# A decoder layer on one core: PSUM banks of the late steps, and the places of the router's parts and of a batch's first scores

## The chip, the cores and the metric

The kernel runs on one core of a Trainium2 chip, as one program. The metric is the device time of one execution in microseconds (us); lower is better. The engines are TensorE (PE in the profile; PEld is its weight load), VectorE (DVE), ScalarE (ACT), GpSimd (POOL) and SyncE (SP), which issues the DMAs. PSUM, in which PE writes and from which DVE and ACT read, has eight banks of 512 fp32 per partition; the kernel holds them as `bank[:, 0..7, :]`.

## What is computed

One layer over 8 sequences ("batches") of 512 rows by 256 features, each with a context of 1024 rows by 128:

```python
x = layernorm(x + attn(x))              # conv over the sequence, 16 heads, softmax of 512x512 scores in bf16
x = layernorm(x + xattn(x, ctx))        # 16 heads: causal self attention + cross attention to ctx, fp32
x = layernorm(x + ffn(x))               # a router over 64 tiles:
#   cluster = argmax(calibrate(x @ cluster_sigs.T)); tile = argmax(calibrate(x @ sigs.T)[cluster])
#   comp = tanh(gelu(x @ cw1 + cb1) @ cw2 + cb2)
#   hh = relu(comp @ w1[tile] + b1[tile]); mag = hh @ w2[tile] + b2[tile]
#   y = layernorm(x + mag * directions[tile] * scale) * gamma + beta
```

## The kernel before

Each engine runs its own program, written out by hand; semaphores tie them. A batch b goes through the stages below, and batches follow one another in a loop (batches 1 to 5 share one body). The router of a batch runs inside the next one (c = b - 1); `tail` does it for the last. What an engine does, and in which order, is the order of the calls in its `batch`.

**Opening: first attention, heads h = 0 to 15.** PE makes four score tiles a head (`scores1`, banks 0 to 3), DVE copies them with their minimum (L712), ACT takes the exps (`exp1`, L565), DVE and ACT scale rows (`norm1`), a DMA transposes them (`transpose1`), PE multiplies with the values (`pv1`, five heads later). `keep_clock` issues filler matmuls (L1263) that nobody reads. Among the heads lie the end of the previous batch (y's transposes `heads_to_features` L1170, the output projection `second_out`, the second norm), the router's first part (`tokens_to_features`, `route`, ACT's `gate_exps` and `hidden`), the context's keys and values (`context_key`, `values`), and DVE's convolution for batch b + 1 (`convolve`, L674 to L679).

**Transition and lead.** Output projection, first norm, the first matmuls of batch b + 1, then twelve projections `unit(u)` for the 16 self and cross heads (four groups of four heads), and between them the first seven sets of row maxima, m = 0 to 6. DVE does the router's gates and choices here.

**Steps s = 0 to 47.** Step s is a block of 128 keys for a group of four heads: 16 self steps, then 32 cross steps. In a step PE issues four transposed scores (`scoresT`, L1402, L1405; one for each row group of 32), ACT takes their exps (L617), and every four steps PE multiplies a "burst" with the values (`pv`, L1420); from burst 9 on it is cut in halves, behind steps s % 4 = 2 and s % 4 = 0. DVE finds the row maxima (`maxima`, L976, L979) some steps ahead, adds them as a row to the queries (`put_rows`, L1001), and copies and divides the results (`outputs` L991, L994; `finish` L1009 to L1015). The maxima end with step 36; the steps from there on are called the late stretch here.

**Banks in the steps.** Banks 0 to 3 are a ring for all that DVE reads: `slot_uses` numbers the uses in PE's order, use n lies in bank n % 4, and PE may write it when use n - 4 is released (`slot_out`). Banks 4 to 7 are ACT's: score n lies in bank 4 + n % 4, and PE waits until exp n - 4 is out (`pT_ready`).

**The router's last part.** `expert_columns` (PE transposes the chosen experts behind step 35, DVE copies them), `gather` behind step 40 (PE: compression L1204, parameters L1208, directions L1213), DVE's `compressed`, ACT's tanh (`compress`), DVE's `spline` (L841 to L852), the norms (`third_sums` to `last_norm`), and SP's `store`. Its scratch lies in q_s and k_s, and so ACT's first projection waits for the previous store (`out_dma`). Behind the last step stand three filler matmuls (L1462).

## Time and profile before

| | us |
|---|---|
| median of 3 runs | 2655.57 |
| lowest and highest | 2650.71, 2660.38 |
| the profiled execution | 2660.13 |
| its span, first to last instruction | 2658.0 |

Busy in the span: PE 2439.8 us (92%), DVE 1924.3 (72%), ACT 1364.6 (51%), POOL 193.6 (7%). The mean granted clock of PE is 0.948. In the timelines, a row gives the start from the span's first instruction, the time to the end of the last of its x instructions, the engine and line, output <- inputs, shape, and in brackets how long the engine stood before it and what released it. An fp32 matmul has two records, so four scores are "x8". Line numbers are those of the kernel before, in `order` rows of the changed kernel those of the changed one.

### The profile page before, as it was taken

Reading aid. Unit: us, or ns where it says so; the run is one execution under the profiler, and the core shown is the slowest. Engines: PE = TensorE matmul, PEld = TensorE weight load, DVE = VectorE, ACT = ScalarE, POOL = GpSimd, SP = SyncE. Lnnn points to the kernel's source line nnn. Section 1 sums busy time; section 2 is a strip of 40 time slices with the busy share of each in tenths; the row PEclk is TensorE's granted clock in tenths of the full one; section 3 lists DMA queues with packets and bytes.
Section 4 is the critical chain, followed back from the end, with each engine's and each line's share of the span. In section 5 each row is a group of like instructions: output and inputs, shape, how many; then the busy total and the mean of one; then the engine's idle time right before and its main releaser. Section 6 shows DMA issues by size and latency. Waiting matters only on the chain.

```text
span 2658.0 us, 44424 instructions
## 1 busy us (share of the span) xinstructions
PE 2439.8 (92%) x13522; PEld 1148.8 (43%) x13554; DVE 1924.3 (72%) x5302; ACT 1364.6 (51%) x2937; POOL 193.6 (7%) x353
## 2 busy tenths in 40 slices
PE   6999989999999989999899998999989999879994
PEld 2454334543445433454335543355434444334432
DVE  6868477884878858687587866878578785668854
ACT  3635564454734648246482465734556355654550
POOL 2010001100011000110001100010000100001000
PEclk8999999998999989999899998999989998999985
DMA  5400032000520006000050001500024000330000
GB/s 138 84 9 1 1 81 55 1 1 9 96 40 1 2 9 119 17 2 1 20 117 9 2 1 47 90 9 1 1 49 79 9 1 1 68 60 1 1 9 8
DMA packets 250899, 83.20 MB, mean 31 GB/s; under 512 B 236064, under 2 KB 246432, under 8 KB 250656
## 3 DMA queue, kind: packets, MB, share of 16 engines
q1 hardware_dynamic: 250656, 80.20, 14.8%
q8 instruction: 123, 2.02, 0.3%
q14 instruction: 120, 0.98, 0.1%
HBM read 17.27 MB, written 4.19 MB: 8 GB/s over the span
## 4 chain that ended last, share of the span: by engine, by line
PE 79%; DVE 11%; issue 4%; ACT 3%; DMA 2%; DVEq 0%; POOL 0%; SPq 0%; ACTq 0%; POOLq 0%
PE bank L1371 18%; PE bank L1131 14%; PE bank L1420 12%; PE bank L1405 10%; PE bank L1367 4%; PE bank L1402 4%; DVE work L712 3%; PE bank L1263 3%; PE bank L1240 2%; PE bank L1227 2%; PE bank L1293 2%; PE bank L1384 2%; DMA work<-work 1%; PE bank L1431 1%; ACT work L617 1%
## 5 line engine op out<-in xcount | busy, mean ns | idle before, releaser
L617 ACT ACTIVATE work<-bank 128x512 f32<-128x512 f32 (+3 forms) x1536 | 744.0, 552 | 669.6 <-PE bank L1405 335.1
L979 DVE TENSOR_REDUCE top_half<-bank 128x1 f32<-128x512 f32 x1024 | 625.6, 682 | 18.5 <-PE bank L1371 18.5
L1371 PE MATMUL bank<-k_c,q_c 32*128 32x512 f32 x2048 | 630.5, 631 | 0.0
L1405 PE MATMUL bank<-q_c,k_c 32*128 32x512 f32 x2048 | 584.4, 656 | 23.2 <-ACT work L617 22.3
L565 ACT ACTIVATE work<-work,neg 128x512 bf16<-128x512 bf16 x512 | 362.2, 711 | 25.5 <-DVE work L712 24.6
L1371 PEld LDWEIGHTS bank<-k_c,q_c 32*128 32x128 f32 x2048 | 273.1, 183 | 226.8 <-DVE top_half L979 140.6
L712 DVE TENSOR_SCALAR_CACHE_REDUCE work<-bank 128x512 bf16<-128x512 f32 x512 | 322.0, 686 | 60.6 <-PE bank L1227 60.5
L1420 PE MATMUL bank<-work,v_flat 128*32 128x512 f32 (+3 forms) x3072 | 341.8, 583 | 19.1 <-ACT work L617 17.3
L1405 PEld LDWEIGHTS bank<-q_c,k_c 32*128 32x128 f32 x2048 | 245.5, 188 | 131.1 <-ACT work L617 70.5
L976 DVE CUSTOM_DVE_ANT_0 masked<-bank,mask_w 128x384 bf16<-128x384 f32 (+3 forms) x512 | 222.7, 488 | 67.3 <-PE bank L1367 60.1
L1402 PE MATMUL bank<-q_s,k_s 32*128 32x512 f32 (+3 forms) x1024 | 261.5, 468 | 0.0
L1420 PEld LDWEIGHTS bank<-work,v_flat 128*32 128x32 f32 x3072 | 91.7, 114 | 261.3 <-issue 149.0
L1367 PE MATMUL bank<-k_s,q_s 32*128 32x128 f32 (+3 forms) x1024 | 183.2, 475 | 0.0
L1227 PE MATMUL bank<-k,q 32*128 32x512 bf16 x512 | 144.9, 388 | 27.2 <-DVE work L712 20.8
L1402 PEld LDWEIGHTS bank<-q_s,k_s 32*128 32x128 f32 x1024 | 145.1, 183 | 13.3 <-ACT work L617 7.6
L1263 PE MATMUL bank<-k,identb 128*128 128x512 bf16 x544 | 145.7, 406 | 2.8 <-issue 1.6
L1240 PE MATMUL bank<-work,v 128*32 128x512 bf16 x512 | 133.5, 383 | 15.8 <-DMA work<-work 14.0
L994 DVE TENSOR_TENSOR featA<-bank,featA 128x512 f32<-128x512 f32 x32 | 22.1, 692 | 167.9 <-PE bank L1420 154.7
L1367 PEld LDWEIGHTS bank<-k_s,q_s 32*128 32x128 f32 x1024 | 100.1, 183 | 76.5 <-DVE top_s L976 32.9
L903 DVE TENSOR_SCALAR work<-work,rden 128x512 bf16<-128x512 bf16 x400 | 120.9, 360 | 4.5
L504 POOL TENSOR_SCALAR_AFFINE_SELECT work<-work 128x512 f32<-128x512 f32 x128 | 81.6, 637 | 557.3 <-ACT work L617 557.3
L991 DVE COPY featA<-bank 128x512 f32<-128x512 f32 x64 | 44.3, 692 | 104.6 <-PE bank L1420 104.3
(201 smaller groups left out, 2499.7 us busy)
## 6 DMA issues: line engine op xcount, KB each, us to landing
xT_pad<-xT SPq DMA_DIRECT2D x16, 256.0 KB, 2.8
ctx_sb<-ctxT SPq DMA_DIRECT2D x8, 512.0 KB, 3.5
x_res<-x SPq DMA_DIRECT2D x8, 512.0 KB, 4.9
out<-k_s SPq DMA_DIRECT2D x8, 512.0 KB, 2.9
work<-work SPq DMA_TRANSPOSE x112, 4.3
qk_sb<-qkT SPq DMA_DIRECT2D x1, 512.0 KB, 4.7
wq_sb<-Wq SPq DMA_DIRECT2D x1, 512.0 KB, 6.6
wk_sb<-Wk SPq DMA_DIRECT2D x1, 512.0 KB, 7.0
```

The costliest lines, as they stand in the source:

```text
L565: nc.scalar.activation(e1[:, h % E1_SLOTS, t, :], s1[:, h % 2, t, :], ACT.Exp, bias=neg1[:, h % 2, t:t + 1], scale=-1.0, accum_out=den1[:, ...
L617: nc.scalar.activation(pT[:, s % PT_SLOTS, g, q0:S], bank[:, RING + n % EXP_RING, 0:S - q0], ACT.Exp, scale=SCALE).then_inc(pT_ready, 1)
L712: nc.vector.tensor_scalar(s1[:, h % 2, t, :], bank[:, (NT * h + t) % A1_BANKS, :], -SCALE, None, ALU.mult, ALU.min, accum_out=neg1[:, h % ...
L976: nc.vector.tensor_tensor_reduce(masked[:, g, 0:n], scores[:, 0:n], mask_w[:, S - n:S], -1.0, -MASKED, ALU.add, ALU.min, top_s[:, i % 2, u ...
L979: nc.vector.tensor_reduce(top_half[:, i % 2, g, u // 2, u % 2:u % 2 + 1], scores, AX.X, ALU.max, negate=True).then_inc(slot_out, 1)
L1131: last = mm(dst, lhsT(k), rhs(k), start=(k == 0), stop=(k == tiles - 1))
L1263: mm(bank[:, at, :], identb[:], k_1[:, 0, :], start=True, stop=True)
L1367: mm(dst[:, 0:n], q_s[rows, i, P * u:n], k_s[rows, i, 0:n], start=True, stop=True, tile_position=(GW * g, 0)).then_inc(slot_in, 1)
L1371: mm(dst, q_c[rows, i, P * t:P * (t + 1)], k_c[rows, i, S * half:S * (half + 1)], start=True, stop=True, tile_position=(GW * g, 0)).then_i ...
L1402: mm(dst[:, 0:S - q0], k_s[rows, i, q0:q0 + P], q_s[rows, i, q0:S], start=True, stop=True, tile_position=(GW * g, 0)).then_inc(sT_mm, 1)
L1405: mm(dst, k_c[rows, i, P * u:P * (u + 1)], q_c[rows, i, :], start=True, stop=True, tile_position=(GW * g, 0)).then_inc(sT_mm, 1)
L1420: last = mm(dst[GW * g:GW * (g + 1), q0:S], v_flat[:, at:at + GW], pT[:, s % PT_SLOTS, g, q0:S], start=(s % BURST == 0), stop=(s % BURST = ...
```

## The change

- From step 37 on (`LATE_STEP`) the ring of DVE is banks 0 and 1 (`LATE_RING`), and the exps use banks 4, 5, 6, 7, 2, 3 (`LATE_EXP_BANKS`, `exp_bank`); `free_slot` and `scoresT` wait accordingly.
- The compression gets a place of its own in the opening: PE at head 8 in bank 5, DVE at 7, ACT's tanh at 9. Expert columns go behind maxima 4 of the lead, the gather and DVE's spline behind maxima 6, the expert choice from maxima 2 to 1. The sums and norms start at step 39. The scratch moves to xs, o1T and r_sb; DVE waits for the store before the second norm, and ACT no longer does.
- A batch opens with the scores of heads 0 and 1; y's transposes, the output projection, the second norm, the router's parts, keys and values follow one or more heads later. The residual is loaded behind head 3. The filler matmuls at a batch's end go; head 7 gets eight fillers instead of four.
- `convolve(b + 2)` stands at step 42 of DVE's program instead of `convolve(b + 1)` in the opening; `convolve(1)` in front of batch 0.

```diff
-    EXPERT_STEP, GATHER_STEP = 35, 40
+    EXPERT_LEAD, GATHER_LEAD = 4, 6
...
+    LATE_STEP = 37
+    LATE_RING, LATE_EXP_BANKS = 2, (4, 5, 6, 7, 2, 3)
...
+        comp = sb("comp", [P, NT, 2])[:]
...
-        z_sb = k_flat[:, 0:NT * D].rearrange("p (t d) -> p t d", t=NT)
+        z_sb = xs_flat.rearrange("p (t d) -> p t d", t=NT)
...
+                if ffn and m == EXPERT_LEAD:
+                    order.append(("expert",))
+                if ffn and m == GATHER_LEAD:
+                    order.extend(("gather", i) for i in range(3))
             for s in range(ALL_STEPS):
+                if s == LATE_STEP:
+                    late = len(order)
...
-                if ffn and s == EXPERT_STEP:
-                    order.append(("expert",))
-                if ffn and s == GATHER_STEP:
-                    order.extend(("gather", i) for i in range(3))
...
-            return {name: n for n, name in enumerate(order)}
+            return {name: n for n, name in enumerate(order)} | {"late": late}
...
+        def slot(uses, use):
+
+            return bank[:, use % RING if use < uses["late"] else (use - uses["late"]) % LATE_RING, :]
...
+        FIRST_LATE = GH * LATE_STEP
+
+        def exp_bank(n):
+            return bank[:, RING + n % EXP_RING if n < FIRST_LATE else LATE_EXP_BANKS[(n - FIRST_LATE) % len(LATE_EXP_BANKS)], :]
...
-                sp.dma_start(out[c].rearrange("(t p) d -> p t d", p=P), z_sb).then_inc(out_dma, 16)
+                sp.dma_start(out[c].rearrange("(t p) d -> p t d", p=P), r_sb[:]).then_inc(out_dma, 16)
...
-                    if h == 1:
+                    if h == 3:
...
-                    if prev:
-                        act.wait_ge(out_dma, FIRST + (b - 1) * 16)
...
-                        nc.scalar.activation(pT[:, s % PT_SLOTS, g, q0:S], bank[:, RING + n % EXP_RING, 0:S - q0], ACT.Exp,
+                        nc.scalar.activation(pT[:, s % PT_SLOTS, g, q0:S], exp_bank(n)[:, 0:S - q0], ACT.Exp,
...
-                if prev:
-                    y_features(0, featA, c)
...
                     if prev:
-                        if h == 2:
+                        if h == 0:
+                            y_features(0, featA, c)
+                        if h == 4:
                             y_features(1, featB, c)
-                        if h == 4:
+                        if h == 5:
                             gate_exps(c)
-                        if h == 5:
+                        if h == 6:
                             hidden(c)
-                    if 0 <= h - 7 < CTX_UNITS:
-                        context_key(h - 7)
+                        if h == 9:
+                            compress(c)
+                    if 0 <= h - 8 < CTX_UNITS:
+                        context_key(h - 8)
...
-                    if prev and s == GATHER_STEP + 2:
-                        compress(c)
...
-            def compressed(c, base, uses):
-                dve.wait_ge(slot_in, base + uses["gather", 2] + 1)
-                nc.vector.tensor_tensor(comp_in, slot(uses["gather", 0])[:, 0:2 * NT].rearrange("p (t i) -> p t i", t=NT),
+                nc.vector.tensor_copy(expertT, slot(uses, use)[0:TILES, :]).then_inc(slot_out, 1)
+
+            def compressed(c):
+                dve.wait_ge(comp_mm, c + 1)
+                nc.vector.tensor_tensor(comp, bank[:, 5, 0:2 * NT].rearrange("p (t i) -> p t i", t=NT),
                                         cb2_row[:].unsqueeze(1).broadcast_to([P, NT, 2]), ALU.add).then_inc(comp_b, 1)
...
-                param = slot(uses["gather", 0])[:, 2 * NT:2 * NT + NT * PARAMS].rearrange("p (t n) -> p t n", t=NT)
+                dve.wait_ge(slot_in, base + uses["gather", 2] + 1)
+                param = slot(uses, uses["gather", 0])[:, 0:NT * PARAMS].rearrange("p (t n) -> p t n", t=NT)
...
                 ln_apply(2, c, lambda t: nc.vector.scalar_tensor_tensor(
-                    z_sb[:, t, :], z_sb[:, t, :], ln_r[:, 2, t:t + 1], r_sb[:, t, :], ALU.mult, ALU.add))
+                    r_sb[:, t, :], z_sb[:, t, :], ln_r[:, 2, t:t + 1], r_sb[:, t, :], ALU.mult, ALU.add))
...
                 scores1(b, 0)
                 scores1(b, 1)
-                if ahead:
-                    convolve(b + 1)
-                if prev:
-                    second_residual(c, sf)
...
                     if prev:
                         if h == 0:
+                            second_residual(c, sf)
+                        if h == 1:
+                            dve.wait_ge(out_dma, FIRST + (b - 1) * 16)
                             second_norm(c)
-                        if h == 5:
+                        if h == 6:
                             router_scores(c)
-                    if h in (6, 8, 10, 12):
-                        values((h - 6) // 2)
+                        if h == 7:
+                            compressed(c)
+                    if h in (7, 9, 11, 13):
+                        values((h - 7) // 2)
...
                     maxima(m)
                     if prev and m == 0:
                         local_gates(c, sf)
-                    if prev and m == 2:
+                    if prev and m == 1:
                         expert_choice(c, sf)
+                    if prev and m == EXPERT_LEAD:
+                        expert_columns(base, uses)
+                    if prev and m == GATHER_LEAD:
+                        spline(c, sf, base, uses)
                 for s in range(ALL_STEPS):
-                    if prev and s == GATHER_STEP + 1:
-                        compressed(c, base, uses)
-                    if prev and s == GATHER_STEP + 2:
-                        spline(c, sf, base, uses)
+                    if prev and s == LATE_STEP + 2:
                         third_sums(c, sf)
-                    if prev and s == GATHER_STEP + 4:
+                    if prev and s == LATE_STEP + 4:
                         third_norm(c)
-                    if prev and s == GATHER_STEP + 5:
+                    if s == LATE_STEP + 5 and ahead == 2:
+                        convolve(b + 2)
+                    if prev and s == LATE_STEP + 6:
                         last_sums(c, sf)
-                    if prev and s == GATHER_STEP + 6:
+                    if prev and s == LATE_STEP + 8:
                         last_norm(c)
...
-                    if prev and s == EXPERT_STEP:
-                        expert_columns(base, uses)
...
+            convolve(1)
             batch(0, prev=False)
...
+            def free_slot(base, uses, use):
+
+                late = uses["late"]
+                if use >= late + LATE_RING:
+                    pe.wait_ge(slot_out, base + use - LATE_RING + 1)
+                elif use >= late:
+                    pe.wait_ge(slot_out, base + late)
+                elif use >= RING:
                     pe.wait_ge(slot_out, base + use - RING + 1)
-                return slot(use)
+                return slot(uses, use)
...
+            def compressed(c):
+                pe.wait_ge(gelu_done, c + 1)
+                for t in range(NT):
+                    last = mm(bank[:, 5, 2 * t:2 * t + 2], hT[:, P * t:P * (t + 1)], cw2_sb[:], start=True, stop=True)
+                last.then_inc(comp_mm, 1)
...
             def gather(c, base, uses):
-                pe.wait_ge(gelu_done, c + 1)
-                dst = free_slot(base, uses["gather", 0])
-                for t in range(NT):
-                    mm(dst[:, 2 * t:2 * t + 2], hT[:, P * t:P * (t + 1)], cw2_sb[:], start=True, stop=True)
+                dst = free_slot(base, uses, uses["gather", 0])
                 pe.wait_ge(slot_out, base + uses["expert",] + 1)
                 for t in range(NT):
-                    at = 2 * NT + PARAMS * t
-                    last = mm(dst[:, at:at + PARAMS], expertT[:, P * t:P * (t + 1)], table[:, D:TABLE], start=True, stop=True)
+                    last = mm(dst[:, PARAMS * t:PARAMS * (t + 1)], expertT[:, P * t:P * (t + 1)], table[:, D:TABLE], start=True, stop=True)
...
                 if prev:
-                    heads_to_features(c)
...
                     elif prev:
-                        pe.wait_ge(gelu_done, b)
+                        pe.wait_ge(comp_b, b)
...
                 scores1(0)
                 scores1(1)
                 if prev:
-                    second_out(c)
+                    heads_to_features(c)
                 keep_clock(7, FILLERS)
                 for h in range(2, H):
                     scores1(h)
                     if h >= 5:
                         pv1(h - 5)
                     if prev:
-                        if h == 3:
+                        if h == 2:
+                            second_out(c)
+                        if h == 5:
                             tokens_to_features(c)
-                        if h == 4:
+                        if h == 6:
                             route(c)
-                    if h in (7, 9, 11, 13):
-                        values((h - 7) // 2)
-                    if 0 <= h - 8 < CTX_UNITS:
-                        context_key(h - 8)
+                        if h == 8:
+                            compressed(c)
+                    if h in (8, 10, 12, 14):
+                        values((h - 8) // 2)
+                    if 0 <= h - 9 < CTX_UNITS:
+                        context_key(h - 9)
                     if h < 13:
-                        keep_clock(7 if h < 4 else 6, FILLERS if h < 7 else FILLERS // 2)
+                        keep_clock(7 if h < 6 else 6, FILLERS if h < 8 else FILLERS // 2)
+                context_key(CTX_UNITS - 1)
...
-                    if n >= EXP_RING:
+                    if n >= FIRST_LATE + len(LATE_EXP_BANKS):
+                        pe.wait_ge(pT_ready, b * ALL_SCORES + n - len(LATE_EXP_BANKS) + 1)
+                    elif n >= FIRST_LATE + EXP_RING:
+                        pe.wait_ge(slot_out, base + uses["late"])
+                    elif n >= EXP_RING:
                         pe.wait_ge(pT_ready, b * ALL_SCORES + n - EXP_RING + 1)
-                    dst = bank[:, RING + n % EXP_RING, :]
+                    dst = exp_bank(n)
...
+                    if prev and m == EXPERT_LEAD:
+                        expert_columns(c, base, uses)
+                    if prev and m == GATHER_LEAD:
+                        gather(c, base, uses)
...
-                    if prev and s == EXPERT_STEP:
-                        expert_columns(c, base, uses)
-                    if prev and s == GATHER_STEP:
-                        gather(c, base, uses)
                 pv(ALL_STEPS // BURST - 1, SECOND_HALF)
                 o_transpose(CROSS, HG - 1)
-                for _ in range(3):
-                    mm(bank[:, 7, :], ident[:], k_c[:, 0, 0:S], start=True, stop=True)
```

Besides, each call of `slot` and `free_slot` gets the table of uses as an argument, and `tail` is reordered alike.

The end of one batch and the opening of the next in PE's program (L1431, L1449: last transposes; L1170, L1178: y's transposes and r_sb's; L1227, L1237: first scores; L1263, L1273: fillers). Before:

```order
L1431 MATMUL bank<-ident,featA 128x128 x4
L1462 MATMUL bank<-k_c,ident 128x512 x3
L1489 REGISTER_ALU
L1489 COMPARE_AND_BRANCH
L1170 MATMUL bank<-ident,y_sb 128x128 x8
L1227 MATMUL bank<-k,q 128x512 x8
L1131 MATMUL bank<-wp_sb,featA 128x256 x8
L1263 MATMUL bank<-k,identb 128x512 x8
L1227 MATMUL bank<-k,q 128x512 x4
L1263 MATMUL bank<-k,identb 128x512 x8
L1227 MATMUL bank<-k,q 128x512 x4
```

Changed:

```order
L1449 MATMUL bank<-ident,featA 128x128 x4
L1506 REGISTER_ALU
L1506 COMPARE_AND_BRANCH
L1237 MATMUL bank<-k,q 128x512 x8
L1178 MATMUL bank<-ident,y_sb 128x128 x8
L1273 MATMUL bank<-k,identb 128x512 x8
L1237 MATMUL bank<-k,q 128x512 x4
L1134 MATMUL bank<-wp_sb,featA 128x256 x8
L1273 MATMUL bank<-k,identb 128x512 x8
L1237 MATMUL bank<-k,q 128x512 x4
L1273 MATMUL bank<-k,identb 128x512 x8
L1237 MATMUL bank<-k,q 128x512 x4
```

The scores of two heads stand ahead of y's transposes, the output projection is behind head 2, the fillers L1462 are gone.

The lead's end in PE's program, between the maxima of set 6 (128x384) and of step 0 (128x512). Before:

```order
L1137 REGISTER_ALU
L1367 MATMUL bank<-k_s,q_s 128x384
L1137 REGISTER_ALU
L1367 MATMUL bank<-k_s,q_s 128x384
L1137 REGISTER_ALU
L1367 MATMUL bank<-k_s,q_s 128x512
L1392 REGISTER_ALU
L1402 MATMUL bank<-q_s,k_s 128x512
L1137 REGISTER_ALU
```

Changed:

```order
L1145 REGISTER_ALU
L1381 MATMUL bank<-k_s,q_s 128x384
L1145 REGISTER_ALU
L1218 MATMUL bank<-table,featB 128x65 x4
L1145 REGISTER_ALU
L1223 MATMUL bank<-table,featB 128x256 x2
L1145 REGISTER_ALU
L1223 MATMUL bank<-table,featB 128x256 x2
L1145 REGISTER_ALU
L1381 MATMUL bank<-k_s,q_s 128x512
L1406 REGISTER_ALU
L1420 MATMUL bank<-q_s,k_s 128x512
```

The gather (L1218, L1223) stands between set 6 and the first maxima of step 0. In DVE's program the spline (here its end, L848 to L852) stands at the same place:

```order
L848 TENSOR_TENSOR o1T<-bank,o1T 128x4
L849 REGISTER_ALU
L850 TENSOR_SCALAR o1T<-o1T,scale_col 128x4
L32 REGISTER_ALU
L852 SCALAR_TENSOR_TENSOR xs<-bank,o1T,r_sb 128x256 x4
L32 REGISTER_ALU
L972 REGISTER_ALU
L977 ISA masked,top_s<-bank,mask_w 128x512
L977 ISA top_s 128x1
```

Step 40 in PE's program: scores, a half burst of values, and what is behind it. Before:

```order
L1405 MATMUL bank<-q_c,k_c 128x512
L1420 MATMUL bank<-work,v_flat 32x512 x8
L1137 REGISTER_ALU
L1204 MATMUL bank<-cw_sb,sig_work 128x2 x4
L1208 MATMUL bank<-table,featB 128x65 x4
L1137 REGISTER_ALU
L1213 MATMUL bank<-table,featB 128x256 x4
L1397 REGISTER_ALU
L1405 MATMUL bank<-q_c,k_c 128x512
L1397 REGISTER_ALU
```

Changed:

```order
L1423 MATMUL bank<-q_c,k_c 128x512
L1429 REGISTER_ALU
L1438 MATMUL bank<-work,v_flat 32x512 x8
L1411 REGISTER_ALU
L1423 MATMUL bank<-q_c,k_c 128x512 x2
L1411 REGISTER_ALU
L1423 MATMUL bank<-q_c,k_c 128x512
L1411 REGISTER_ALU
L1423 MATMUL bank<-q_c,k_c 128x512
```

The gather is gone from there, and of the next step's scores the first two follow each other without a wait of their own.

## Rows read from the trace of the kernel before

**Rows 1.** First line of the profile's page: span and instructions.
```profile
span 2658.0 us, 44424 instructions
```

**Rows 2.** Stretches: length, busy PE, PEld, DVE, ACT, POOL, PE clock, DMA share, GB/s.
```profile
291.00:339.00 48.00, 41.83 (x238) 13.80 (x235) 8.90 (x16) 24.26 (x48) 0.00 (x0) 0.89 0.00 1
...
611.00:664.00 53.00, 47.22 (x248) 17.28 (x241) 19.14 (x54) 22.50 (x45) 2.80 (x4) 0.81 0.03 11
...
1581.00:1630.00 49.00, 42.28 (x252) 15.78 (x242) 19.47 (x54) 22.36 (x46) 2.80 (x4) 0.93 0.03 12
...
458.00:500.00 42.00, 40.99 (x244) 20.95 (x244) 31.13 (x137) 15.70 (x32) 6.56 (x14) 1.00 0.05 14
```

**Rows 3.** Timeline of PE, late stretch of batch 0: start, us, what [idle before].
```profile
301.26 3.23 PE L1420 MATMUL bank<-work,v_flat 128*32 128x512 f32 x16
...
310.67 1.14 PE L1405 MATMUL bank<-q_c,k_c 32*128 32x512 f32 x8
...
312.53 2.59 PE L1405 MATMUL bank<-q_c,k_c 32*128 32x512 f32 x8 [0.73 <-ACT work L617]
...
315.05 1.92 PE L1420 MATMUL bank<-work,v_flat 128*32 128x512 f32 x16
...
334.37 3.39 PE L1420 MATMUL bank<-work,v_flat 128*32 128x512 f32 x16 [2.21 <-ACT work L617]
...
339.05 2.74 PE L1462 MATMUL bank<-k_c,ident 128*128 128x512 f32 x6
```

**Rows 4.** Timeline of ACT, a late cycle of batch 0.
```profile
311.88 4.03 ACT L617 ACTIVATE work<-bank 128x512 f32<-128x512 f32 x8 [2.21 <-PE bank L1405]
```

**Rows 5.** Timelines of DVE and PE: last maxima, and fillers behind a batch.
```profile
291.57 2.48 DVE L979 TENSOR_REDUCE top_half<-bank 128x1 f32<-128x512 f32 x4
...
608.79 2.47 DVE L979 TENSOR_REDUCE top_half<-bank 128x1 f32<-128x512 f32 x4
...
2540.80 2.46 DVE L979 TENSOR_REDUCE top_half<-bank 128x1 f32<-128x512 f32 x4
...
664.07 2.74 PE L1462 MATMUL bank<-k_c,ident 128*128 128x512 f32 x6
...
2594.33 4.43 PE L1462 MATMUL bank<-k_c,ident 128*128 128x512 f32 x6
```

**Rows 6.** Timeline of PE, the gather of batch 1.
```profile
628.20 1.05 PE L1204 MATMUL bank<-cw_sb,sig_work 64*128 64x2 f32 x8
...
629.11 1.08 PE L1208 MATMUL bank<-table,featB 64*128 64x65 f32 x8
...
630.03 2.15 PE L1213 MATMUL bank<-table,featB 64*128 64x256 f32 x8
```

**Rows 7.** Timeline of DVE, the opening of batch 1.
```profile
339.54 0.42 DVE L1011 TENSOR_TENSOR y_tmp<-bank,rec 128x256 f32<-128x256 f32 x1
...
343.02 0.69 DVE L712 TENSOR_SCALAR_CACHE_REDUCE work<-bank 128x512 bf16<-128x512 f32 x1 [2.59 <-PE bank L1227]
...
347.91 0.48 DVE L674 TENSOR_SCALAR xs<-xT_pad,conv_sb 128x512 f32<-128x512 f32 x1
...
351.86 1.28 DVE L742 TENSOR_TENSOR x_res<-x_res,bank 128x512 f32<-128x512 f32 x2
```

**Rows 8.** Timeline of PE, the opening of batch 1.
```profile
357.10 0.38 PE L1227 MATMUL bank<-k,q 32*128 32x512 bf16 x1 [2.93 <-DVE work L712]
...
379.62 1.03 PE L1227 MATMUL bank<-k,q 32*128 32x512 bf16 x4
```

**Rows 9.** Timeline of DVE, first maxima of step 0 in batch 1.
```profile
483.63 0.69 DVE L976 CUSTOM_DVE_ANT_0 masked<-bank,mask_w 128x512 bf16<-128x512 f32 x1
```

**Rows 10.** Timeline of DVE, first and last instruction of batch 1's spline.
```profile
636.41 0.23 DVE L841 TENSOR_TENSOR q_s<-bank,q_s 128x64 f32<-128x64 f32 x1 [4.02 <-ACT q_s L555]
...
638.65 1.66 DVE L852 SCALAR_TENSOR_TENSOR k_s<-bank,q_s,r_sb 128x256 f32<-128x256 f32 x4
```

**Rows 11.** Timeline of PE, the compression behind batch 7.
```profile
2631.64 1.86 PE L1204 MATMUL bank<-cw_sb,sig_work 64*128 64x2 f32 x8
```

59 lines of the change are left out of this document (24 added, 35 removed).

## The prediction

> **What bounds the kernel now.** I read first the page's span, then busy time by stretches, then the timelines of PE, DVE and ACT inside one batch, stage by stage. Eight batches share 2658.0 us [rows 1], one about 323 us. A batch has four stages with different limits. In the opening (16 first heads) PE, DVE and ACT feed each other. In the transition and the lead (projections and the first maxima) PE is the limit until projection 11 is out, then DVE. In steps 0 to 36 DVE's maxima are the limit. In the late stretch, from the last maxima to the end, nobody is full: ACT is busy 24.3 of 48 us in batch 0 and 22.5 of 53 us in batch 1, DVE 8.9 and 19.1, and PE's granted clock (1.00 is 2.4 GHz) falls to 0.89 and 0.81 on average [rows 2]. This is where the change aims, so I read it at single groups.
>
> In batch 0, at full clock, two late steps are a cycle: four scores back to back at 310.67, four more at 312.53 that each wait for a bank (2.59 us instead of 1.14), a half burst of values at 315.05. ACT's eight exps take 4.03 from 311.88 on, after 2.21 of idle: **6.24 us per two steps**, the same in each cycle at full clock [rows 3, 4]. A row group of PE needs about 1.06 us for one score (two passes), four run side by side, so a score that is released late costs its whole length before the values may start.
>
> From the start of the last four maxima to the start of the three L1462 fillers, this stretch is 339.05 - 291.57 = 47.5 us in batch 0, 664.07 - 608.79 = 55.3 in batch 1, 53.5 in batch 7 [rows 3, 5]; over the seven batches that carry the router it is 52.8 on average (50.2 to 55.3).
>
> **The change, part by part.** All per batch; there are seven batches with a router behind them.
>
> *Six banks for the exps.* With six, two of the second four scores start at once, the other two when ACT has freed the banks of the first two: ACT starts 1.21 us after the first score and takes 0.504 per exp [rows 3, 4], so the banks are free at 1.21 + 0.58 + 0.07 = 1.86 and 2.36, and the last score ends at 2.36 + 1.06 = 3.42. The half burst needs the first step's exps, done at 1.21 + 4 x 0.504 + 0.17 = 3.40. So it starts at 3.42 and the next cycle 1.86 later, at **5.28: 0.96 saved** per two steps. Five cycles (steps 37 to 46): **-4.8**. Ends: 0 if the values still start where they did, and 6.24 - 4.03 = 2.2 per cycle (-11) if ACT became the limit, which PE's order doesn't allow. VectorE's two ring banks cost nothing by the order: six ring uses are left, spread over eleven steps, and each finds its predecessor's predecessor copied some 5 us before.
>
> *The router's gather leaves step 40.* In batch 1 PE spends 628.20 to 632.1 on it, in front of the next scores [rows 6]: **-3.9**. The tanh and VectorE's part there lie in idle time.
>
> *The clock.* Where PE has stood or starved, the granted clock halves: the half burst takes 3.23 us at 301.26 against 1.92 at 315.05 [rows 3]. Batch 0 loses 4.2 us to that: 1.3 there and 1.5 in each of its last two half bursts (3.38 and 3.39). So its late stretch at full clock would be 43.3, and with the cycles 38.5. I take 2.1 us as left, for the waits before the last burst (2.2 us of idle, [rows 3]), which stay. So the stretch becomes **40.6**: -12.2 from 52.8, -6.9 in batch 0. The clock's share is about 3.5; the ends are 0 and 5.6 saved.
>
> The Trainium skill ("TensorE: Matmul & The Clock Gate", "A second HAM failure mode: psum-queue depth-cycling") says that cycling through PSUM banks with small idles between matmul groups makes the clock swing. The rows agree in kind: most slow pieces lie in this stretch. Taken fully, it would leave no loss, and the stretch would be 38.5.
>
> *The opening.* Now: last transposes, fillers, y's transposes, scores. DVE's first copy in batch 1 comes 3.06 us after the end of y_tmp (339.54 + 0.42 to 343.02) [rows 7], in the others 3.7 to 4.9. The change puts the scores first, which need only y_tmp: first copy at about +0.9. The convolution (347.91 to 351.86, 3.95 us [rows 7]) leaves DVE's path, and with it a wait of PE of 2.93 us [rows 8]; it lands at step 42, where DVE idles. But PE's list from the first scores to those of head 7 stays some 30 us (7 score groups of 0.96, 6 x 8 fillers of 1.87 per eight, second output 3.8, transposes 2.8, router 3.9, values 1.9), and 5 us of waits among heads 2 to 5 remain, because router and second norm are now one head later in the same chain: head 7 at +35.9, before 379.62 - 339.96 = +39.7 [rows 7, 8]. At its end the last context key now waits for ACT to pass head 14's exps, and gives back 1.4. Compression adds 1.05 on PE, in place of a wait that it fills. Net **-3** in batches 1 to 6, -1 in batch 7 (it had no convolution); ends -6 and +1. In batch 0 the convolution moves in front of the first head: +2.
>
> *The lead.* This is the bill. DVE has no slack once projections are out: from the middle of maxima 5 on its work is back to back, and step 0's maxima start at 483.63 [rows 9]. The change puts there the copy of the expert columns (0.6), and behind maxima 6 the spline, 636.41 to 640.31 = 3.9 us [rows 10]. The gather's second part takes PE 3.2 (1.08 + 2.15 [rows 6]) behind the scores of maxima 6, while DVE has only 1.9 us of maxima to do: DVE idles about 1.9. And step 0's maxima need the slots which the spline empties, so PE can't run ahead. 0.5 + 1.9 + 3.9 + 0.1 = 6.4, less 0.6 for the copy that leaves step 35. PE idles 2 to 4 us there; a piece at half clock after it costs me 1.2. Sum **+7**; ends +4 (the gather hidden) and +21 (below). The earlier expert choice and the dropped wait for the output lie where PE is the limit: 0.
>
> *The end.* After batch 7 the fillers, 4.43 us from 2594.33 on [rows 5], no longer delay y's transposes; y itself is complete some 1.5 us after their start (in batch 0 at 340.4 against 339.05 [rows 3, 7]): -2.8. The compression (2631.64, 1.86 at half clock) goes behind other waits: -1.9; the tanh's exchange -0.3 [rows 11]. **-5**.
>
> Sum: 7 x (-12.2 + 7) - 6.9 + 2 - 19 - 5 = **-65 us**. The profiled execution took 2660.1 us (span 2658.0), the median of the three runs is 2655.6: so 2595 and **2590**.
>
> **The rivals.**
> 1. *The clock holds everywhere* (0.2). Stretch at 38.5 (-14.3), lead at +5.8, opening -4: 7 x -12.5 - 9 + 2 - 5 = -100: 2556. For it: batch 4 had 0.93 there with all its waits [rows 2]. Against: the wait before the last burst stays.
> 2. *The lead eats it* (0.25). The late stretch gives 8 (gather, half the cycle's gain, no clock), the opening 1, the lead costs 7: 7 x -2 - 12 = -26: 2630. If the banks do nothing at all, because the half bursts start where they did, the stretch gives 4.5 and the time is about 2650, within the bound of no change.
> 3. *Slower* (0.05). PE's idle behind the gather halves its clock through steps 0 to 3. PE has no slack there either (busy 41.0 of the 42 us from 458 to 500 [rows 2]), so over the 14.4 us from 483.6 to 498 a halved clock makes it the limit and doubles them: lead +21. Against -15.2 from the rest it is 7 x 6 - 10 = +32: 2688. It decides from a lead cost of about 16.6. Against: the slow pieces of the late stretch are single half bursts with full ones behind them [rows 3].
>
> The skill's same page ("Why this matters for your kernels") advises against gaps between matmul bursts. That speaks against dropping the fillers and against the gather's place; by it, rival 3's piece would appear behind the gather in each batch, while I book 1.2.
>
> **How the numbers follow.** Forecast 0.5, between 2570 and 2615. Rivals as above. The range 2550 to 2640 takes in rival 1 and most of rival 2. A measurement can tell 0.3% (8 us) from no change: faster 0.87, same 0.07, slower 0.06.
>
> **What would show it.** Late cycles: ACT's groups of eight 5.3 us apart instead of 6.24, and two of the second four scores without a wait. Clock in the late stretch above 0.9. In the lead, an idle of DVE of 2 us before the spline and the first step's maxima some 6 us later after the last projection. Head 7's scores 36 us after y_tmp. It is wrong if DVE's late block (third norm, convolution, sums) holds a ring slot for which a half burst waits, or if the last context key delays the transposes by more than 1.4.

## The result, and the profile after

The changed kernel takes 2639.55 us (median of 7 runs, 2633.86 to 2640.67), the kernel before 2660.38 (7 runs beside them, 2650.71 to 2666.49): ratio 0.9919, 95% interval 0.9900 to 0.9938. It is faster by 21 us. I had forecast 65, at 2590; the measured time lies just inside the upper edge of my range.

The profiled execution has a span of 2631.8 us against 2658.0 [rows 1]. Where the 26 us come from, worked out from the timelines of DVE and ACT between fixed events, as a mean over the seven batches that carry a router (us). "y_tmp" is the last of the four in a batch, "the featB copy" is ACT's copy behind the first attention. The late stretch ends here at y_tmp; in the prediction it ended at the fillers, about 1 us earlier.

| stage | before | after | forecast of the change |
|---|---|---|---|
| opening: end of y_tmp to the featB copy | 105.3 | 108.5 | -3 |
| transition, to the first maxima | 13.6 | 13.5 | 0 |
| lead: first maxima to first cross maxima | 46.6 | 55.1 | +7 |
| steps, to the last top_c | 105.5 | 105.2 | 0 |
| late stretch, last top_c to the end of y_tmp | 51.3 | 36.7 | -12.2 |
| sum of one batch | 322.2 | 319.1 | -8.2 |
| all of batch 0 | 340.0 | 332.3 | -4.9 |
| behind batch 7 | 62.7 | 66.0 | -5 |

7 x (-3.1) - 7.7 + 3.3 = -26. The late stretch gained more than forecast, the lead cost more, and the opening and the program's end went the other way.

**The late stretch.** Stretches of the changed kernel (columns as in [rows 2]): the late stretches of batches 0, 1 and 4, and the lead of batch 1.

```profile
292.30:332.30 40.00, 36.20 (x244) 12.02 (x236) 14.09 (x26) 24.26 (x48) 0.00 (x0) 1.00 0.04 14
608.40:649.10 40.70, 36.91 (x244) 12.25 (x237) 23.11 (x55) 24.26 (x48) 2.79 (x4) 0.95 0.09 28
1575.60:1616.90 41.30, 37.50 (x244) 12.13 (x236) 23.04 (x55) 24.26 (x48) 2.79 (x4) 0.96 0.08 27
448.70:490.00 41.30, 39.77 (x174) 20.72 (x175) 28.43 (x119) 11.33 (x21) 6.85 (x17) 0.88 0.05 14
```

The granted clock there was 0.89, 0.81 and 0.93 [rows 2] and is 1.00, 0.95 and 0.96; the lead stood at 1.00 before and is now at 0.88. ACT's timeline in the late stretch of batch 2:

```profile
947.24 4.03 ACT L616 ACTIVATE work<-bank 128x512 f32<-128x512 f32 x8 [1.76 <-PE bank L1423]
952.44 4.03 ACT L616 ACTIVATE work<-bank 128x512 f32<-128x512 f32 x8 [1.18 <-PE bank L1423]
957.64 4.03 ACT L616 ACTIVATE work<-bank 128x512 f32<-128x512 f32 x8 [1.18 <-PE bank L1423]
962.84 4.03 ACT L616 ACTIVATE work<-bank 128x512 f32<-128x512 f32 x8 [1.18 <-PE bank L1423]
```

Groups of eight start 5.20 us apart, with 1.18 of idle instead of 2.21 [rows 4]: forecast 5.28 instead of 6.24. In the late stretches of the seven router batches before, late scores waited 30 times for ACT to free a bank, 19.6 us in all; in the changed kernel one such wait of 0.2 is left, and PE waits nowhere there for a ring slot.

**The seam between batches.** PE's timeline from batch 2 to 3 (the loop jumps there) and from 5 to 6 (the loop is left); y_tmp ends at 974.38 and 1937.75:

```profile
972.98 0.65 PE L1449 MATMUL bank<-ident,featA 128*128 128x128 f32 x4 [0.89 <-DVE featA L995]
976.92 3.83 PE L1237 MATMUL bank<-k,q 32*128 32x512 bf16 x8 [3.29 <-issue]
980.68 1.97 PE L1178 MATMUL bank<-ident,y_sb 128*128 128x128 f32 x8
982.44 3.62 PE L1273 MATMUL bank<-k,identb 128*128 128x512 bf16 x8
...
1937.81 3.62 PE L1237 MATMUL bank<-k,q 32*128 32x512 bf16 x8 [0.81 <-DVE y_tmp L1012]
```

At the jump PE stands 2.5 us longer and waits for nothing that the profile shows ("issue"). In both places the scores and what follows run at half clock: eight scores take 3.83 and 3.62 (four at full clock: 1.03), fillers that take 1.9 take 3.62.

**The lead.** PE and DVE around the gather, batch 3:

```profile
1121.02 1.10 PE L1218 MATMUL bank<-table,featB 64*128 64x65 f32 x8
1121.96 2.80 PE L1223 MATMUL bank<-table,featB 64*128 64x256 f32 x8
1124.69 1.22 PE L1381 MATMUL bank<-k_s,q_s 32*128 32x512 f32 x1
1124.80 0.23 DVE L841 TENSOR_TENSOR o1T<-bank,comp 128x64 f32<-128x64 f32 x1 [2.47 <-PE bank L1223]
```

DVE idles 2.47 us (1.6 to 1.7 in batches 2, 6 and 7, 2.8 to 3.0 in 1, 4 and 5; forecast 1.9), and the scores behind it take 1.22 instead of 0.69. Of the lead's +8.5, some 4.5 lie in front of the first exps (L616) and 4 between these and the first cross maxima (22.0 to 26.1 on average, the granted clock there 1.00 to 0.85). That second piece, in batches 2 and 3:

```profile
801.60:833.30 31.70, 30.70 (x175) 20.27 (x176) 21.32 (x83) 12.57 (x30) 4.45 (x7) 0.68 0.00 1
1126.80:1151.80 25.00, 25.00 (x175) 16.41 (x176) 20.32 (x79) 12.39 (x30) 4.44 (x7) 0.87 0.01 1
```

The other five batches have a clock of 0.87 to 0.89 there. Batch 2 goes the way of my rival 3, in one batch of seven: a clock of 0.68 makes that piece 31.7 us instead of 25.

**Behind batch 7.** PE's second output, and DVE up to the local gates:

```profile
2569.10 5.91 PE L1134 MATMUL bank<-wp_sb,featA 128*128 128x256 f32 x16 [1.10 <-ACT featA L539]
...
2587.99 0.42 DVE L751 COPY sig_raw<-bank 128x256 f32<-128x256 f32 x1 [7.25 <-ACT gates L543]
2592.82 0.17 DVE L825 TENSOR_TENSOR comp<-bank,cb_row 128x8 f32<-128x8 f32 x1 [4.41 <-PE bank L1211]
2599.70 0.18 DVE L765 TENSOR_SCALAR gates<-gates 128x32 f32<-128x32 f32 x1 [0.39 <-ACT gates L548]
```

DVE now waits 4.41 us for the compression in front of the cluster gates. The second output starts 3.3 us after y_tmp instead of 5.5, and loses that again: 5.91 us instead of 3.69.

### The profile page after: what moved, and what is told of

Same layout as the page of the kernel before. It is cut to its first block, busy times and chain, and to the rows that moved or that the text cites. A ratio compares the mean times of both kernels' runs of the same rounds, so it can differ in the third digit from the quotient of the medians.

```text
span 2631.8 us, 44428 instructions
## 1 busy us (share of the span) xinstructions
PE 2424.1 (92%) x13538; PEld 1145.0 (44%) x13538; DVE 1930.6 (73%) x5302; ACT 1366.1 (52%) x2937; POOL 192.9 (7%) x353
## 4 chain that ended last, share of the span: by engine, by line
PE 79%; DVE 10%; ACT 5%; issue 5%; DVEq 0%; DMA 0%; ACTq 0%; POOL 0%; SPq 0%; POOLq 0%
PE bank L1385 18%; PE bank L1134 15%; PE bank L1438 12%; PE bank L1423 9%; PE bank L1381 5%; PE bank L1420 3%; PE bank L1273 3%; PE bank L1237 3%; ACT work L566 3%; DVE work L711 3%; PE bank L1250 3%; PE bank L1302 2%; PE bank L1449 1%; PE bank L1398 1%; PE bank L1178 1%
## 5 line engine op out<-in xcount | busy, mean ns | idle before, releaser
L616 ACT ACTIVATE work<-bank 128x512 f32<-128x512 f32 (+3 forms) x1536 | 745.4, 552 | 620.0 <-PE bank L1420 323.0
L1423 PE MATMUL bank<-q_c,k_c 32*128 32x512 f32 x2048 | 553.0, 630 | 0.2 <-ACT work L616 0.2
L1438 PE MATMUL bank<-work,v_flat 128*32 128x512 f32 (+3 forms) x3072 | 319.6, 551 | 17.4 <-ACT work L616 17.3
L1420 PE MATMUL bank<-q_s,k_s 32*128 32x512 f32 (+3 forms) x1024 | 288.7, 522 | 0.0
L1423 PEld LDWEIGHTS bank<-q_c,k_c 32*128 32x128 f32 x2048 | 229.2, 183 | 96.9 <-ACT work L616 63.0
L1381 PE MATMUL bank<-k_s,q_s 32*128 32x128 f32 (+3 forms) x1024 | 217.1, 514 | 4.2 <-DVE o1T L848 3.1
L1237 PE MATMUL bank<-k,q 32*128 32x512 bf16 x512 | 155.3, 404 | 41.9 <-DVE work L711 21.0
L1420 PEld LDWEIGHTS bank<-q_s,k_s 32*128 32x128 f32 x1024 | 159.3, 202 | 15.6 <-ACT work L616 7.1
L1273 PE MATMUL bank<-k,identb 128*128 128x512 bf16 x608 | 164.7, 413 | 0.0
L1381 PEld LDWEIGHTS bank<-k_s,q_s 32*128 32x128 f32 x1024 | 115.8, 201 | 90.2 <-issue 38.0
```

Source lines behind the costliest of these rows:

```text
L616: nc.scalar.activation(pT[:, s % PT_SLOTS, g, q0:S], exp_bank(n)[:, 0:S - q0], ACT.Exp, scale=SCALE).then_inc(pT_ready, 1)
L1237: mm(bank[:, n % A1_BANKS, :], q_1[rows, i, P * t:P * (t + 1)], k_1[rows, i, :], start=True, stop=True, tile_position=(GW * (h % GH), 0)). ...
L1273: mm(bank[:, at, :], identb[:], k_1[:, 0, :], start=True, stop=True)
L1381: mm(dst[:, 0:n], q_s[rows, i, P * u:n], k_s[rows, i, 0:n], start=True, stop=True, tile_position=(GW * g, 0)).then_inc(slot_in, 1)
L1420: mm(dst[:, 0:S - q0], k_s[rows, i, q0:q0 + P], q_s[rows, i, q0:S], start=True, stop=True, tile_position=(GW * g, 0)).then_inc(sT_mm, 1)
L1423: mm(dst, k_c[rows, i, P * u:P * (u + 1)], q_c[rows, i, :], start=True, stop=True, tile_position=(GW * g, 0)).then_inc(sT_mm, 1)
```

## The experiments

Each was timed in three rounds beside the kernel before; the profiles are compared stage by stage as above. The runs of one kernel lie 1.4 to 25 us apart, so a difference of medians under some 10 us counts only with the stages beside it. All medians (us), and ratios to the kernel before with 95% intervals:

| run | what it is | median | ratio |
|---|---|---|---|
| e1 | change without the six banks | 2697.8 | 1.0145 (1.0113 to 1.0176) |
| e2 | change with the old opening | 2606.0 | 0.9806 (0.9775 to 0.9838) |
| e3 | before, new opening, early compression and late convolution | 2662.3 | 1.0013 (1.0001 to 1.0025) |
| e4 | change, fillers at the batch's end | 2641.6 | 0.9937 (0.9904 to 0.9970) |
| e5 | e2, convolution in the opening | 2613.0 | 0.9841 (0.9800 to 0.9883) |
| e6 | change, last context key later | 2630.5 | 0.9900 (0.9862 to 0.9937) |
| e7 | change, loop written out | 2633.0 | 0.9898 (0.9863 to 0.9933) |
| e8 | e2, router's last part late in three pieces | 2551.0 | 0.9602 (0.9561 to 0.9643) |
| e9 | e8, keys and values one head later | 2566.0 | 0.9647 (0.9627 to 0.9667) |
| e10 | e8, no fillers at the batch's end | 2557.1 | 0.9616 (0.9595 to 0.9636) |
| e11 | e2, spline waits for the first piece only | 2570.5 | 0.9673 (0.9647 to 0.9699) |
| e12 | e8, convolution in the opening | 2562.7 | 0.9633 (0.9609 to 0.9658) |
| e13 | e8, whole new opening | 2591.4 | 0.9745 (0.9709 to 0.9780) |
| e14 | e8, first half of the new opening | 2563.7 | 0.9636 (0.9599 to 0.9673) |
| e15 | e8, scores ahead of y's transposes | 2563.6 | 0.9646 (0.9611 to 0.9681) |
| e16 | e8, compression late behind batch 7 | 2545.2 | 0.9577 (0.9542 to 0.9612) |

### What each of the three parts is worth: e1, e2, e3, e12

e1:
```diff
-            return {name: n for n, name in enumerate(order)} | {"late": late}
+            return {name: n for n, name in enumerate(order)} | {"late": 10**9}
-        FIRST_LATE = GH * LATE_STEP
+        FIRST_LATE = 10**9
```

> The changed kernel with VectorE's ring of four and ScalarE's four banks to the end; opening and lead as changed. In the traces of before and after, the stretch from the last top_c to the end of y_tmp fell from 51.3 to 36.7 us per router batch. If the six banks carry their 4.8 us of it and nothing else (theory), the stretch is 41.5 and the time 2639.6 + 8 x 4.8 = 2678 us. If the banks also carried what the granted clock gave back there (rival 1), the stretch is about 47 and the time about 2720. If the gather's leaving and the quieter queue did all of it (rival 2), the stretch stays at 37 to 38 and the time at 2640 to 2648.

Measured 2697.8, +58 us or 7.3 per batch. The late stretch is 45.3 us against 36.7 with the banks, the clock there 0.89 to 0.92; opening and lead are the same (108.6 and 54.5). The 8.6 of the late stretch lie between theory (4.8) and rival 1: the banks give the cycle's 5 us and carry the clock with them. This kernel is slower than the one before: without its banks the change loses.

e2 (PE's part; DVE, ACT and the residual's load follow):
```diff
-                    pe.wait_ge(slot_out, base)
+                    heads_to_features(c)
+                    pe.wait_ge(slot_out, base)
...
                 scores1(1)
                 if prev:
-                    heads_to_features(c)
+                    second_out(c)
...
-                        if h == 2:
-                            second_out(c)
-                        if h == 5:
+                        if h == 3:
                             tokens_to_features(c)
-                        if h == 6:
+                        if h == 4:
                             route(c)
...
-                    if 0 <= h - 9 < CTX_UNITS:
-                        context_key(h - 9)
+                    if 0 <= h - 8 < CTX_UNITS:
+                        context_key(h - 8)
```

> The changed kernel with the opening in the old order (y's transposes ahead of the scores, second output behind two heads, second norm, router, values, context keys and compression one head earlier, the three fillers back at the batch's end, output store and residual load as before); late banks, router in the lead and the late convolution stay. The traces say that the new opening cost about 3.2 us per router batch against the old one, and the program's end 3.3. Theory (the new order itself lengthens the opening): 2639.6 - 7 x 3.2 - 3.3 = 2614 us, and up to 4 us less per batch since the convolution stays out of it: 2590 to 2614. Rival (the order is innocent: half clock moved from the late stretch into whatever comes next): 2636 to 2650, with a granted clock below 0.85 in the first 20 us of the openings here too.

Measured 2606.0 (runs from 2588.1, the profiled one, to 2613.3): theory. The opening is 102.5 us, 5.9 shorter than the new one; the late stretch stays at 36.7 and the lead at 55.0. The first 20 us of the openings are at 0.91 to 0.97, not below 0.85 (the changed kernel: 0.74 to 0.83). So it is the new order that brings the half clock, and not the late stretch that hands it on.

e3, the kernel before with the new opening and the convolution at step 41. The compression comes with the opening, so the gather of step 40 is without it, and so are DVE's and ACT's programs there:

> The kernel before with the new opening and the late convolution alone: four and four banks, expert columns at step 35, gather at step 40. My forecast had this part at -3 us per router batch, -5 at the end, +2 in batch 0: 2636 us. Theory from the traces (the new order costs 3.2 per batch and 3.3 at the end): 2660.4 + 7 x 3.2 + 3.3 + 2 = 2688. Rival (interaction: the opening is only bad behind a late stretch at full clock, or the late fillers kept a clock that is lost now): between, about 2660.

Measured 2662.3. That is neither my -25 nor +28: the opening takes 108.5 us here as well, +3.2, so its price does not depend on the banks or the lead. But the late stretch went from 51.3 to 47.8 (clock 0.88 to 0.93, instead of 0.81 to 0.93). The edit does touch it: from the gather's first matmul to the next scores PE now takes 2.8 us instead of 3.9, since the compression is gone,

```profile
631.47 1.10 PE L1226 MATMUL bank<-table,featB 64*128 64x65 f32 x8
632.41 1.94 PE L1231 MATMUL bank<-table,featB 64*128 64x256 f32 x8
634.28 1.14 PE L1431 MATMUL bank<-q_c,k_c 32*128 32x512 f32 x8
```

and the scores behind it are at full clock here (1.14, batch 1), where before they took 2.09. The other 2.4 us were not taken apart.

e12, and with it what the banks do alone (the gather cut in three, see e8):
```diff
-                    if s == 39 and ahead == 2:
-                        convolve(b + 2)
...
                 scores1(b, 1)
+                if ahead:
+                    convolve(b + 1)
```

> The kernel with the router's last part late (2551 us) with the convolution back in the opening: against the kernel before, only the six late banks (with the gather in three pieces, which two ring banks need) and the compression in the opening are left. Theory (moving the convolution was worth 7 us, 2613 against 2606): 2558. Rival (2.7 us in six batches, as the stage lengths of the kernel before against the late-convolution kernel say): 2567. Rival 2 (the late DVE block without the convolution lets the half bursts start earlier): 2551 or less.

Measured 2562.7: 98 us less than before by the banks, the cut gather with its early spline, the early compression and the expert choice alone, late stretch 39.5. Against e8 the convolution's move is worth 12 us here, with the intervals of the ratios overlapping, and 7 in the pair e5 and e2. By the stages the gain is not where I had put it: the opening is 104.2 against 103.9, the late stretch 39.5 against 38.2.

> As the kernel with the old opening (2606 us), and the convolution back between the first two heads' scores: late banks and the router in the lead alone are left of the change. From y_tmp to the featB copy the kernel before takes 105.3 us, that kernel 102.5. Theory (parts add up; moving the convolution alone is worth 2.7 us in six batches, and a little in batch 0): 2606 + 17 = 2623, opening at 105.3 again. Rival (the convolution in the late stretch slows that stretch as much as it frees the opening): 2606.

Measured 2613.0, opening 105.0 (before: 105.3). The stage lengths say 2.5 per batch, the medians 7 in all, with e2's runs 25 us apart. Both pairs have the sign of a gain; its size is known only within 7 to 15, and it lies in the opening in this pair and in the late stretch in the other.

### The opening: e9, e13, e14, e15, e6, e4, e7, e10

These stand on e8, where lead and steps are undisturbed. e13 is e8 with the opening of the change.

> The kernel with the router's last part late (2551 us) and the whole new opening. It is the reference for the next run, and asks whether the new opening costs the same without the router in the lead. Theory (its price is its own: 108.5 us from y_tmp to the featB copy in three kernels with different ends of the batch before): 108.5 here too, 2551 + 7 x 4.5 = 2583. Rival (its price hangs on a disturbed clock that the lead brings): below 105, 2560 or less.

Measured 2591.4, +40; opening 108.8 against 103.9. Theory: the price is its own. In the profiles (+43) the openings make 34 of it, the late stretches 7 and batch 0 another 5.

> The kernel with the router's last part late (2551 us), and of the changed opening only its second half: compression, values and context keys one head later, one more group of full fillers, the last context key behind the loop of heads. Theory (that half carries most of the 5.9 us per router batch by which the new opening is longer: about 2.5 between heads 8 and 15 and 2.5 in PE's wait in front of the last key): featB copy at +108 instead of +103.9, 2551 + 8 x 4.5 = 2587. Rival (the first half, scores ahead of y's transposes and second output behind head 2, carries it): 2551 to 2560.

Measured 2566.0, +15; opening 105.1. The second half alone costs 1.1 us per batch, not 4.5, and 4.9 once in batch 0: the theory fell.

e14 against e13:
```diff
-                        if h == 5:
+                        if h == 4:
                             tokens_to_features(c)
-                        if h == 6:
+                        if h == 5:
                             route(c)
...
-                context_key(CTX_UNITS - 1)
```

> As the run before, but y's second transposes, router, compression, values and context keys one head earlier again; what is left of the new opening is its first half: scores ahead of y's transposes, second output behind head 2, second residual and norm behind heads 0 and 1, no fillers at the batch's end. Keys and values alone had cost 15 us (1.1 us per batch in the profiles). Theory (from head 5 on PE also has the values of the first heads to do and is the limit, so that transposes and router at heads 5 and 6 cost their full 5.3 us, while at heads 3 and 4 they fill waits of PE for DVE; one head earlier takes back about a third of it, the second output's 3.8 behind head 2 stays): 106, 2568. Rival 1 (only the order at the start counts): 107 to 108, 2575 to 2583. Rival 2 (only the second half counts): 104, 2553.

Measured 2563.7, +12.7; opening 105.3 (+1.4), a little better than the theory's 106. So the two cost 1.1 and 1.4 alone, and the whole 4.8: 15 + 13 us against 40. They are not quite halves of it, though: transposes and router stand at heads 3 and 4 in e8 and e9, at 4 and 5 in e14, and at 5 and 6 only in e13. Whether the missing 2.3 are that last step or the two delays acting on each other, no run separates. Batch 3 of e8, PE around the transposes and the router at heads 3 and 4 (batch begins at 948.16):

```profile
966.24 0.38 PE L1256 MATMUL bank<-k,q 32*128 32x512 bf16 x1 [0.17 <-DVE work L720]
...
969.37 1.09 PE L1195 MATMUL bank<-ident,r_sb 128*128 128x128 f32 x8 [0.91 <-DVE r_sb L734]
970.30 1.89 PE L1292 MATMUL bank<-k,identb 128*128 128x512 bf16 x8
972.12 0.82 PE L1256 MATMUL bank<-k,q 32*128 32x512 bf16 x3
973.14 0.39 PE L1256 MATMUL bank<-k,q 32*128 32x512 bf16 x1 [0.21 <-DVE work L720]
973.46 2.00 PE L1151 MATMUL bank<-sigT,featB 128*128 128x72 f32 x16
```

and of e13 at heads 5 and 6 (begins at 963.84):

```profile
990.19 0.38 PE L1256 MATMUL bank<-k,q 32*128 32x512 bf16 x1 [1.12 <-DVE work L720]
...
992.34 1.75 PE L1269 MATMUL bank<-work,v 128*32 128x512 bf16 x4
994.02 1.97 PE L1195 MATMUL bank<-ident,r_sb 128*128 128x128 f32 x8
995.78 1.97 PE L1292 MATMUL bank<-k,identb 128*128 128x512 bf16 x8
997.68 1.03 PE L1256 MATMUL bank<-k,q 32*128 32x512 bf16 x4
998.64 1.04 PE L1269 MATMUL bank<-work,v 128*32 128x512 bf16 x4
...
1001.54 1.93 PE L1151 MATMUL bank<-featB,cw_sb 128*64 128x512 f32 x4
1003.41 1.90 PE L1292 MATMUL bank<-k,identb 128*128 128x512 bf16 x8
```

In e8 PE waits for DVE (0.17 to 0.91 us) up to the router. In e13 the last such waits are in front of head 5 (1.12, then 0.23 before each of its other scores); from there PE has the values of head h - 5 (L1269) too, and nothing is free until head 8. From DVE's copy of head 2 to that of head 7 it takes 29.6 us instead of 21.6 (batch 3), of which 3.7 are the second output, which in e8 lies in front of head 2. That eats the earlier start (copy of head 2 at +12.2 instead of +17.3), and head 7 is 2.9 later.

I read this as: in e8 transposes and router fill waits, in e13 they count in full. The account of PE's time shows something else as larger. Stretches of PE alone (length, busy PE, granted clock, DMA share, GB/s), batch 3, from the end of y_tmp to DVE's copy of head 7, in the kernel before, the changed one, e8 and e13:

```profile
985.06:1025.33 40.27, 36.92 (x141) 0.87 0.46 90
974.39:1016.18 41.79, 36.59 (x138) 0.84 0.37 77
948.16:987.04 38.88, 35.75 (x143) 0.91 0.44 80
963.84:1005.66 41.82, 36.29 (x138) 0.84 0.37 77
```

The same for whole openings, mean of seven batches (us). "Lost to half clock" is half of PE's busy time in which the granted clock was 0.5, an estimate of what full clock would have saved on PE; the last column is what is left, PE's list at full clock:

| kernel | opening | PE idle | lost to half clock | list at full clock |
|---|---|---|---|---|
| before | 105.3 | 11.2 | 5.6 | 88.5 |
| changed | 108.5 | 11.3 | 9.3 | 87.8 |
| e2 | 102.5 | 10.2 | 2.3 | 90.0 |
| e8 | 103.9 | 9.5 | 4.7 | 89.8 |
| e9 | 105.1 | 10.1 | 5.6 | 89.3 |
| e14 | 105.3 | 10.4 | 7.3 | 87.5 |
| e13 | 108.8 | 11.6 | 9.4 | 87.7 |

From e8 to e13 half clock takes 4.7 us more, idle 2.1 more (part of it the jump, below), and the list is 2.1 shorter; from e2 to the changed kernel it is 7.0, 1.1 and -2.2. So the price of the new opening is for the most part PE's work at half clock. That it comes with the order is shown by e2 and e13; by which of the moves the clock falls is not.

> The kernel with the router's last part late (2551 us), with the first two heads' scores ahead of y's transposes and no fillers at the batch's end, but second output right behind those transposes and everything after it in the old place. Leaving only the fillers out had given 2557. Theory (the scores' place is not what the new opening costs; it is what stands behind heads 2 to 6): 104 to 105, 2551 to 2560. Rival (the place of the scores costs the clock, and all that follows): 107 or more, above 2570.

Measured 2563.6 (+12.6), opening 105.4: just above the theory's opening, 4 us above its time, far from the rival. Putting the scores first gains nothing even with all else in place, and the first 20 us have here the lowest clock of all kernels (0.66 to 0.74), so that clock alone does not make the price either.

> The changed kernel with the last context key behind the tile transposes of head 14 instead of in front of them. In the trace after, PE waits 2.58 us there for ScalarE's copy of the key before and then spends 1.1. Theory (this wait delays the transposes and all behind them, some 2.5 of the 5.9 us by which the new opening is longer than the old): 2639.6 - 8 x 2.5 = 2620. Rival (ScalarE, which has to pass the same exps for its half of the transposes, is late anyway): 2636 to 2640.

Measured 2630.5, 9 us less instead of 20, with overlapping intervals. The wait in front of the last key is real (2.58 us of PE in batch 6 of the changed kernel, released by ACT's copy of the key before), but costs at most about 1 per batch: the opening is 0.4 shorter (108.0). Between the two.

> The changed kernel with eight filler matmuls (1.9 us at full clock) behind the last output transpose of each batch, in front of the next batch's scores. In the trace after, PE starts those scores 2.5 us after y_tmp in the four batches entered by the loop's jump, with nothing to wait for, and at half clock in all seven (3.6 to 3.8 us for eight). Theory (PE's idle there costs the clock, and the jump runs beside queued fillers): scores take 2.0, granted clock of the first 20 us from 0.77 to above 0.9, 2 us per batch less and 2.5 more in four of them: 2639.6 - 14 - 10 = 2616, at least 2626. Rival (fillers only push the scores back): 2640 to 2650, clock as before.

Measured 2641.6: the rival. The clock of the first 20 us rises only from 0.78 to 0.85 on average, the first copy behind the jump still comes 3.1 to 3.5 us after y_tmp, and the opening grows by 1.6.

e7, in PE's program; the other four engines' loops are written out alike:
```diff
-            with pe.Fori(1, B - 2) as b:
+            for b in range(1, B - 2):
```

> The changed kernel with batches 1 to 5 written out instead of looped. In the trace after, PE starts the first scores 2.5 us after y_tmp in the four batches that are entered by the loop's jump, with nothing to wait for, and 0.06 after it elsewhere. Theory (the jump itself costs that and the new order has nothing queued to hide it): first copy at +0.6 in every batch, 2639.6 - 10 = 2630. Rival (new code has to be brought in either way): the delay stays or spreads, 2638 to 2660.

Measured 2633.0, the sign of the theory at two thirds of its size, with overlapping intervals. The first copy is at +0.5 in every batch, so the jump costs 2.6 us at that point; but the opening ends only 0.6 earlier on average (107.9). The start is not slack: DVE's copy of head 7 is still 2.1 us earlier on average (+38.2 against +40.4). It is lost behind that, where 10.2 us instead of 6.8 stand at half clock, worth some 1.7 on PE.

> The kernel with the router's last part late (2551 us) without the three fillers at a batch's end, so that y's transposes can start as soon as y is complete. In the old-opening traces they start 3.2 us after y is ready. Theory (the start of the opening is on the path): 7 x 2.5 = 17 us less, and the end of the program 3 less: 2531. Rival 1 (PE's clock falls without them and the first heads take it back, as the new opening shows at 0.74 to 0.83 in its first 20 us): 2545 to 2560. Rival 2 (the start is slack; the written-out kernel began every batch 2.6 us earlier and won only 6 in all): 2548 to 2551.

Measured 2557.1: rival 1 by the time, 6 us more, where single runs just overlap (e8 2547.0 to 2557.6, this 2556.7 to 2559.8). Five of the seven openings have their first 20 us at 0.74 (e8: 0.83 in six, 0.96 in one); the opening is 104.0, as in e8. The late stretches are 39.4 instead of 38.2, and behind batch 7 it is 3.9 less, so the 6 us do not come out of the openings. What the Trainium skill advises ("TensorE: Matmul & The Clock Gate", "Why this matters for your kernels"), to leave no gaps between bursts of matmuls, agrees here with the clock of the first heads, but in the opening's length the fillers neither cost nor gain; in e4, where the same idea was applied in front of the new opening, they gained nothing.

### The lead: e8, e11

e11:
```diff
                 dve.wait_ge(comp_done, c + 1)
-                dve.wait_ge(slot_in, base + uses["gather", 2] + 1)
+                dve.wait_ge(slot_in, base + uses["gather", 0] + 1)
...
                 do(nc.vector.tensor_scalar(mag, mag, scale_col[:, 0:1], None, ALU.mult))
+                dve.wait_ge(slot_in, base + uses["gather", 2] + 1)
```

> The kernel with the old opening and the router in the lead (2606 us); the spline's first part waits only for the gather's first piece and the blend with r for the last two, so that DVE works while PE gathers. In the traces DVE idles 1.6 us there at full clock and 2.5 to 2.8 where the gather runs at half clock. Theory (the idle is one of the lead's terms, as forecast at 1.9): lead 55.0 to 53.2, 2606 - 7 x 1.8 = 2593. Rival (the scores of step 0 are late anyway, because they need the slots that the blend empties and run at half clock): 2600 to 2606.

Measured 2570.5, 35 us less than e2 (18 by the two profiles, since e2's profiled run was its fastest). The lead is 52.7 instead of 55.0, and none of that is in front of the first exps (29.7 in both); the piece behind, from first exps to cross maxima, falls from 25.2 to 23.0, its clock from 0.87 on average to 0.96. DVE starts the spline without a wait, and waits a shorter time later:

```profile
782.47 0.22 DVE L841 TENSOR_TENSOR o1T<-bank,comp 128x64 f32<-128x64 f32 x1
...
785.99 1.66 DVE L853 SCALAR_TENSOR_TENSOR xs<-bank,o1T,r_sb 128x256 f32<-128x256 f32 x4 [1.32 <-PE bank L1224]
```

So what the idle of 1.7 to 3.4 us (e2) cost lay behind it, in PE's work at a lower clock, and not in front of the first exps.

e8 (order of ring uses; DVE and PE follow it):
```diff
-    EXPERT_LEAD, GATHER_LEAD = 4, 6
+    EXPERT_STEP, GATHER_AT = 35, (37, 40, 41)
...
                 order.extend(("o",) + part for part in outputs_behind(s))
+                if ffn and s == EXPERT_STEP:
+                    order.append(("expert",))
+                if ffn and s in GATHER_AT:
+                    order.append(("gather", GATHER_AT.index(s)))
```

> The kernel with the old opening, late banks and late convolution (2606 us), and the router's last part out of the lead again: expert columns at step 35, the gather in three pieces behind steps 37, 40 and 41, so that two ring banks are enough, the spline behind step 37, the blend with r in two halves behind 40 and 41, the convolution at step 39. Theory (the lead's 8.4 us per batch come from the spline, the wait for the gather and the clock behind it; in the late stretch PE pays 3.3 us of gather and DVE is idle half the time): 2606 - 7 x (8.4 - 3.3) = 2570, and the stretch from the first maxima to the first cross maxima at 46.6 again. Rival 1 (two ring banks make the half bursts wait for the spline, or the clock falls there): the late stretch at 45, time 2606 or more. Rival 2 (the lead's loss is not the router's): lead stays at 55.

Measured 2551.0: 55 us less than e2 by the medians and 35 by the two profiles (e2's was its fastest run), where the theory had 36. It is the best of these kernels but one. The lead is 46.6 us again, and the late stretch 38.2 instead of 36.7. PE in batch 1, and that stretch:

```profile
603.36 1.10 PE L1236 MATMUL bank<-table,featB 64*128 64x65 f32 x8
...
613.74 1.13 PE L1242 MATMUL bank<-table,featB 64*128 64x256 f32 x4
...
615.87 1.13 PE L1242 MATMUL bank<-table,featB 64*128 64x256 f32 x4
```

```profile
599.90:637.90 38.00, 34.58 (x239) 12.61 (x232) 23.31 (x61) 22.41 (x44) 2.80 (x4) 1.00 0.09 30
```

3.4 us of gather cost 1.5: the rest lies in time in which PE waited for exps. At step 40 of the kernel before, in one block together with the compression (1.05), it had taken 3.9 [rows 6]. One block in this place, with six banks, was not tried; so how much of the gain is the cutting and how much the banks is open.

### The program's end: e16

```diff
                 hidden(c)
-                compress(c)
                 local_exps(c)
+                compress(c)
...
                 router_scores(c)
-                compressed(c)
                 cluster_gates(c, sf)
...
                 expert_choice(c, sf)
+                compressed(c)
```

> The kernel with the router's last part late (2551 us); only behind the last batch the tanh comes after the local gates' exps, and VectorE's part of the compression after the expert choice. In the traces with the change, VectorE waits 4.4 us for the compression in front of the cluster gates, and from the router's scores to the local gates it is 11.7 us instead of 7.3. Theory (that wait is why the end of the program grew instead of shrinking by 5): end from y_tmp 64.1 to 59.7, 2547. Rival (the wait comes back behind the expert choice): 64, 2551.

Measured 2545.2, 6 us less, with overlapping intervals; the stage says it more firmly: from y_tmp to the end 56.9 instead of 64.1 in the profiles, of which the moved wait explains 4.4; the other 2.8 were not followed, and e12, whose end is that of e8, has 62.2 there. Its ratio to the kernel before is 0.9577 (0.9542 to 0.9612).

## Why the prediction was wrong

- **Six banks, right.** Cycle 5.20 us (forecast 5.28); no half burst waits for the ring of two. e1 puts banks and clock at 8.6 per batch, where I had 4.8 + 3.5.
- **The late stretch, a gain under-sized.** -14.6 instead of -12.2: I kept 2.1 us of half clock for the waits before the last burst. The waits are there (2.13 us), the half clock behind them in only some batches. This is the effect that the Trainium skill describes ("TensorE: Matmul & The Clock Gate", "A second HAM failure mode: psum-queue depth-cycling") and that I had beside it; the trace agrees: the stretch with fewer small waits stands at 0.95 to 1.00. My rival 1 was right for this stage.
- **The opening, the step that failed.** Forecast -3, measured +3.2: 41 us in seven batches (22 instead of -19), as much as the whole miss of 39. The step is "head 7 at +35.9": I had summed PE's list to there at full clock (some 30 us) with 5 us of waits and the start of 0.9, and compared it with the +39.7 of the kernel before, which holds time at half clock. DVE's copy of head 7 came at +38.2 to +42.1, +40.4 on average (its scores start 0.4 before). The list was right, 30.3 us at full clock, and idle is less than booked, 4.0 with the start in it. What I had put at nothing, without a reason, is the clock: PE works at half clock long enough on the way to lose 6.0 us (3.8 before). Behind head 7 the opening takes 68.1 us instead of 65.1, where I had +1.4: half clock 1.5 more, the four added fillers 1.0, idle 0.5. That the new order brings this is shown (e2, e13). That transposes and router went from heads where PE waits for DVE to heads where PE is full fits the rows of e8 and e13, but explains at most the smaller part; why the clock falls stays open. "If the last context key delays the transposes by more than 1.4" was the wrong alarm: e6 gives at most about 1 per batch. The convolution's move was a gain (e5; in e12 it shows in the late stretch, not in the opening), and the new order itself costs 4.8 to 5.9.
- **The lead, right in kind, under-sized.** +8.5 instead of +7. Idle 1.6 to 3.0 (1.9), copy and spline as summed; the piece behind it took 4.0 more, where I had booked 1.2 for half clock (0.87 to 0.89 from first exps to cross maxima, in one batch 0.68). What I did not see is that 2.3 of it come from one wait placed too early in front of the spline (e11), and that the late stretch, once it has six banks, has room for the whole gather at 1.5 (e8).
- **The end, the wrong sign.** -5 forecast, +3.3 measured. "The compression goes behind other waits" was read from PE's list only. On DVE, it stands in front of the cluster gates, and DVE waits 4.41 for it (e16). The earlier second output was taken back by the clock (5.91 us instead of 3.69). Together that is 6.6 of the miss of 8.3; the rest was not followed.
- **Batch 0**: -7.7 instead of -4.9, its late stretch at a clock of 1.00.
- **The number near my rival 2** (2630) is luck: it had 8 us from the late stretch, which gave 14.6, and 1 from the opening, which took 3.2. That the time lies in the range at all comes from that rival too.

## What to carry to other kernels

A sum of an engine's list has to say at which clock it runs. Before comparing it with a measured time, take that time apart into idle, work at half clock and work at full clock, and give each of the three a forecast; here the list came out within 1 us and idle within 2, and the clock, left out, was the miss. An operation that is moved has to be looked up in the queue of every engine that touches it, in the tail as in the loop. And before a block is moved out of a stage to make room, try to cut it into pieces with a wait each: the gather in three pieces cost 1.5 us near where it was, with six banks, against 8.5 elsewhere.

## What the runs showed of the hardware

- The jump back of a hardware loop leaves PE idle: 3.29 us with no releaser where a seam without a jump shows 0.81; written out, the first copy comes at +0.5 instead of +3.2. Of the four gains of 2.6 us the whole kernel keeps 6.5 us by the medians (e7); the rest goes to more work at half clock later in the opening.
- PE's list of an opening, about 90 us at full clock in both, loses 2.3 us to half clock in one order (e2) and 9.3 in another (the changed kernel), with PE's idle time at 10.2 and 11.3.
- The granted clock ties stages together. In e11 the time behind a removed idle fell and not the idle's own place, and the same code ran a lead at 0.68 in batch 2 and at 0.87 to 0.89 in its neighbours. Which of two equal batches falls to half clock could not be told from what stood before it; it stays open.
- Kernels differ in spread: e2's four runs lie 25 us apart, e6's 1.4. A comparison with e2 rests on both its median and its stages for that reason.
